# One stage program, a transfer in place of a shift matmul, and new engine orders in a local transformer on one Trainium2 core

## The reference, cut to what matters

```
def shift_tokens(t):
    a, s = jnp.split(t, 2, -1)
    s = jnp.pad(s, ((0, 0), (1, 0), (0, 0)))[:, :-1]
    return jnp.concatenate([a, s], -1)
...
for i in range(DEPTH):          # 6
    x = attn_layer(shift_tokens(x), Wqkv[i], q_scale[i], k_scale[i], Wo[i]) + x
    x = ffn_layer(shift_tokens(x), ln_g[i], ln_b[i], W1[i], b1[i], W2[i], b2[i]) + x
```

## Time and profile before

| what | value |
|---|---|
| median of 3 runs | 2609.49 us (2609.47 to 2609.76) |
| the profiled execution's own time | 2604.96 us |
| its span | 2603.1 us |
| PE busy in the span | 96% |
| DVE, ACT, POOL busy | 74%, 68%, 57% |
| granted TensorE clock, mean | 0.983 |

### The profile page before, as it was taken

How to read it: one execution, slowest core, us unless ns; L and a number is a source line. 1 busy time by engine, 2 the same in 40 slices (tenths; PEclk the granted TensorE clock), 3 DMA queues, 4 the chain that set the end, 5 groups by cost and what they waited for, 6 DMA issues and landing times.

```text
span 2603.1 us, 102870 instructions
## 1 busy us (share of the span) xinstructions
PE 2496.2 (96%) x41090; PEld 1928.4 (74%) x41090; DVE 1934.7 (74%) x4711; ACT 1771.4 (68%) x3770; POOL 1491.5 (57%) x1917
## 2 busy tenths in 40 slices
PE   8899999999999999999999999999799988999898
PEld 6667777777677777777677777777698967999667
DVE  6778788888878878788888878887456877555564
ACT  6677777777777778777777777777454357333465
POOL 5566677677666676676677677667332056000572
PEclk9999999999999999999999999999899989999999
DMA  3200000110011100110010100000002000000022
GB/s 94 67 19 12 16 16 15 33 32 21 19 26 29 32 19 19 32 34 17 19 33 25 29 19 16 14 16 16 4 5 88 0 5 6 2 0 1 13 78 82
DMA packets 56424, 66.72 MB, mean 26 GB/s; under 512 B 25113, under 2 KB 31076, under 8 KB 55652
## 3 DMA queue, kind: packets, MB, share of 16 engines
q1 hardware_dynamic: 56292, 64.88, 9.0%
HBM read 38.23 MB, written 1.05 MB: 15 GB/s over the span
## 4 chain that ended last, share of the span: by engine, by line
PE 85%; issue 5%; DVE 4%; POOL 4%; ACT 3%; DVEq 0%; DMA 0%; SPq 0%; POOLq 0%; ACTq 0%
PE ps L797 13%; PE ps L902 7%; PE ps L818 6%; PE ps L811 6%; PE ps L845 5%; PE ps L882 5%; PE ps L924 5%; PE ps L859 3%; PE ps L936 3%; PE ps L892 3%; PE ps L1016 3%; PE ps L1000 3%; PE ps L1001 3%; PE ps L742 2%; PE ps L752 1%
## 5 line engine op out<-in xcount | busy, mean ns | idle before, releaser
L1192 ACT ACTIVATE area<-ps 128x512 f32<-128x512 f32 (+4 forms) x1520 | 770.0, 536 | 380.2 <-PE ps L788 109.6
L1670 POOL TENSOR_TENSOR area<-area 128x512 f32<-128x512 f32 x384 | 481.9, 1276 | 8.2 <-DVE area L2149 8.2
L1692 POOL TENSOR_TENSOR area<-area,mx 128x512 f32<-128x512 f32 x192 | 200.2, 1043 | 489.2 <-DVE mx L2177 489.2
L797 PE MATMUL ps<-lw,area 128*128 128x512 f32 x768 | 413.2, 620 | 1.5 <-ACT area L1192 1.1
L1684 POOL TENSOR_TENSOR area<-area,rnq 128x512 f32<-128x512 f32 x384 | 392.5, 1043 | 7.5
L1315 ACT ACTIVATE area<-ps 128x512 f32<-128x512 f32 x384 | 227.1, 591 | 89.9 <-PE ps L797 89.8
L2147 DVE TENSOR_TENSOR area<-ps,table 128x512 f32<-128x512 f32 x384 | 260.9, 679 | 8.2 <-ACT area L1315 5.0
L2149 DVE TENSOR_TENSOR area<-ps,table 128x512 f32<-128x512 f32 x384 | 261.5, 681 | 0.0
L2128 DVE TENSOR_REDUCE ssq<-area 128x8 f32<-128x512 f32 x384 | 252.2, 677 | 1.7 <-ACT area L1315 0.8
L811 PEld LDWEIGHTS ps<-ident,area 128*128 128x128 f32 x1536 | 180.6, 142 | 65.0 <-issue 53.1
L811 PE MATMUL ps<-ident,area 128*128 128x128 f32 x1536 | 218.4, 275 | 10.6 <-POOL area L1684 7.7
(11 more groups left out here) (300 smaller groups left out, 5607.6 us busy)
## 6 DMA issues: line engine op xcount, KB each, us to landing
lvm<-area SPq DMA_DIRECT2D x384, 65.0 KB
lw<-in_wqkv SPq DMA_DIRECT2D x36, 256.0 KB
area<-in_moe_w SPq DMA_DIRECT2D x24, 256.0 KB, 2.7
lw<-in_wout SPq DMA_DIRECT2D x12, 256.0 KB
ctxT<-in_ctxT SPq DMA_DIRECT2D x64, 38.5 KB, 1.8
lw<-in_moe_w SPq DMA_DIRECT2D x8, 256.0 KB, 2.8
lw<-in_wff SPq DMA_DIRECT2D x6, 341.0 KB
lw<-in_moe_g SPq DMA_DIRECT2D x1, 1152.0 KB
```

Source lines behind the costliest of these rows:

```text
L797: nc.tensor.matmul(banks[:, lb_qk[j], :], xsT[s], wqkv[w.p][:, j * 512:(j + 1) * 512], start=True, stop=True).then_inc(l_qk_ps, 1)
L1192: return nc.scalar.activation(dst, src, ACT.Identity if kw else ACT.Copy, **kw)
L1670: pool.tensor_tensor(QR[s][:, cols], QR[s][:, cols], RA[s][:, cols], ALU.add).then_inc(l_rsum, 1)
```

## The change

It has five parts.

1. The token shift of the feed-forward half is no longer two matmuls. `y1` gets 64 more columns (`ysh`), and SP copies y1's features 64 to 127 of tokens 0 to 126 into these columns one partition lower: an SBUF to SBUF DMA of 127 rows of 256 bytes, which waits for y1. Row 0 is zeroed once.
2. The statistics read `ysh` in SBUF. The normalisation moves from DVE to ACT as one activation with scale 1/deviation and bias -mean/deviation; DVE makes that bias with a one-column instruction (`norm_shift`).
3. The orders in `stages` of PE, ACT, DVE and POOL and the PSUM banks are new; on POOL, `rotary_sum` and `normalised` of a unit move from its b call to its a call, as does `queries_keys_T` 2 on ACT.
4. The gated addition after the local transformer is split: sequences 0 and 1 first, the other 14 inside the first stage of the next attention.
5. Three of the `late_prep` instructions move ahead of the first mixture, behind a wait for all late loads; the preparations of w3 and w3o move into the last quad of the second mixture.

```
-        lb_tokens, lb_qk, lb_qkT, lb_v = 3, (4, 3, 4, 0), (3, 0, 2, 5), (1, 5)
+        lb_tokens, lb_qk, lb_qkT, lb_v = 0, (0, 7, 4, 2), (7, 6, 5, 7), (3, 6)
...
+        def shifted_tokens(s):
+            return ysh[s].rearrange("p (k n) -> p k n", n=64)[:, 0:3:2, :]
...
+            def shifted_tokens(s, unit):
+
+                sp.wait_ge(l_y1, unit + 1)
+                sp.dma_start(ysh[s][1:S, D:D + 64], y1[s][0:S - 1, 64:D]).then_inc(l_sh_ps, 16)
+
+            def stages(a, b, c):
+                if a:
+                    middle_values(*a)
+                    shifted_tokens(*a)
...
-            def shift_back(s, w):
-                pe.wait_ge(l_y1, nth(0, w.it, s))
-                nc.tensor.matmul(banks[:, lb_shift, 0:64], ident[:, :], y1[s][:, 0:64], start=True, stop=True)
-                nc.tensor.matmul(banks[:, lb_shift, 64:128], shift[:, :], y1[s][:, 64:128],
-                                 start=True, stop=True).then_inc(l_sh_ps, 1)
...
+            def shifted_normed(s, w):
+                act.wait_ge(l_nb, nth(0, w.it, s))
+                copy(xn[s][:, :].rearrange("p (k n) -> p k n", n=64), shifted_tokens(s), scale=rs[s][:, 0:1],
+                     bias=nrm[s][:, 0:1]).then_inc(l_xn, 1)
...
             def shifted_stats(s, w):
-                dve.wait_ge(l_sh_ps, nth(0, w.it, s))
-                V.bn_stats(st[s][:, 0:6], banks[:, lb_shift, 0:D]).then_inc(l_st, 1)
+                dve.wait_ge(l_sh_ps, 16 * nth(0, w.it, s))
+                V.bn_stats(st[s][:, 0:6], shifted_tokens(s)).then_inc(l_st, 1)
...
-            def shifted_normed(s, w):
+            def norm_shift(s, w):
+                dve.wait_ge(l_mv, nth(0, w.it, s))
                 dve.wait_ge(l_rs, nth(0, w.it, s))
-                V.tensor_scalar(xn[s][:, :], banks[:, lb_shift, 0:D], mv[s][:, 0:1], rs[s][:, 0:1],
-                                ALU.subtract, ALU.mult).then_inc(l_xn, 1)
+                V.scalar_tensor_tensor(nrm[s][:, :], mv[s][:, 0:1], -1.0, rs[s][:, :], ALU.mult, ALU.mult).then_inc(l_nb, 1)
...
+                    if b is None and c is None:
+                        gated(slice(G, B))
...
             attention(XA[1], 1)
-            mixture(MOE[0])
             dve.wait_ge(late_loaded, 288)
             V.tensor_tensor(side[:, :], side[:, :], side[:, :], ALU.add).then_inc(late_prep, 1)
...
+            mixture(MOE[0])
```

More of the change, by code:

```diff
@@ L543, in middle_values, with three @@
                     sp.dma_start(LVM[s][at + 32:at + 64, :, :], LV[s][at + 32:at + 64, 0, :, :]).then_inc(l_vm, 16)
-            def layer(l):
-                with sp.Fori(0, IT) as pr:
-                    for s in range(G):
-                        middle_values(s, l * B + pr * G + s)
+            def shifted_tokens(s, unit):
[5 more added lines that the diff above has]
+                    shifted_tokens(*a)
+            def three(s, unit):
+                stages((s, unit), (1 - s, unit - 1), (s, unit - 2))
             def layer_and_next_weights(l, p):
@@ L559, in layer_and_next_weights @@
                             sp.dma_start(dst, src).then_inc(lw_loaded[p], 16)
-            layer(0)
+            stages((0, 0), None, None)
+            stages((1, 1), (0, 0), None)
+            with sp.Fori(0, IT - 1) as pr:
+                for s in range(G):
+                    three(s, pr * G + G + s)
             with sp.Fori(0, DEPTH // 2 - 1) as lp:
@@ L564, in _ @@
                 layer_and_next_weights(lp * 2 + 2, 1)
-            layer(DEPTH - 1)
+            with sp.Fori(0, IT) as pr:
+                for s in range(G):
+                    three(s, (DEPTH - 1) * B + pr * G + s)
+            stages(None, (1, DEPTH * B - 1), (0, DEPTH * B - 2))
+            stages(None, None, (1, DEPTH * B - 1))
             contexts(1)
@@ L861, in probs_T, with probs_values @@
                 last.then_inc(l_pT_ps, 1)
[L863 removed]
+            def probs_values(s, w, m, near=None):
                 if m == 0:
@@ L987, in quad_logits, with output_shift, output_means @@
                 last.then_inc(r_lg_ps, 1)
+            def output_shift():
+                pe.wait_ge(m_rw, 2 * B - 3)
+                for c in range(4):
+                    last = nc.tensor.matmul(later[:, 0, 0:D], ob[:, c:c + 1].to_broadcast([D, S]), w3o[:, c, :], start=(c == 0), stop=(c == 3))
+                last.then_inc(t_prep_ps, 1)
+            def output_means():
+                pe.wait_ge(t_prep, 3)
+                for c in range(4):
+                    last = nc.tensor.matmul(later[:, 1, 0:D], mean512[:, :], w3o[:, c, :], start=(c == 0), stop=(c == 3))
+                last.then_inc(t_prep_ps, 1)
             def mixture(m):
@@ L1128, in stages @@
                     if b: outputs(*b)
-                def gain_sums():
-                    pe.wait_ge(t_prep, 3)
-                    for c in range(4):
-                        last = nc.tensor.matmul(ps[1][:, 2, 0:D], mean512[:, :], w3o[:, c, :], start=(c == 0), stop=(c == 3))
-                    last.then_inc(t_prep_ps, 1)
                 def up(b):
@@ L2232, in stages @@
                 if a: tokens(*a)
+                if b:
+                    masked(*b, 0)
+                    maxima(*b, 0)
                 if c:
@@ L2319, in halves @@
                         residual(*b)
+                        if m["n"] and ahead is None: output_weights(b[0])
                 dve.wait_ge(x_updated, G + m["ln"])
```

372 lines of the change are left out of this document (192 added, 180 removed).

## The result

The change makes the kernel 1.4% faster, a little under half of what was forecast: a median of 2573.63 us (2572.11 to 2573.84, 3 runs) against 2609.49, a ratio of 0.9863 (95% interval 0.985 to 0.9876), 35.9 us less. The forecast was 2533.

The account below looks back on a forecast made before the run. PE (TensorE) was taken to bound the local transformer's units: -0.53 - 0.29 + 0.05 = -0.77 us a unit, -73.2 over 95 distances; with the ends -76.8 in total, forecast 2533 us, range 2512 to 2572.

Parts of the forecast that it names:

- Two shift matmuls, -0.53: PE in the steady unit: removing the two shift matmuls saves their issue time, 0.53 us a unit.
- Tile shapes, -0.29: PE in the steady unit: fewer entries to and exits from small-tile groups save 0.29 us a unit, bounds 0 and -0.4.
- Waits, +0.05: PE in the steady unit: waits of 0.32 us after the change against 0.27 before, so +0.05 a unit.
- The two chains that I walked: PE's waits in the new order: probs_T 1 behind scores 1, 0.21 us; scores 0 behind queries_keys_T 0, 0.11 us.
- Loop ends and layer borders, which the change leaves alone: Local transformer: the 0.19 us by which the mean distance of 17.66 exceeds the 17.47 unit stays as it was.
- Transfer, 3.5 us, free: Shift DMA from y1 to shifted_stats: takes 3.5 us and costs nothing, since up to about 3.8 us is covered.
- SP's order, nothing: SP's queue: the four value transfers now wait behind the new transfer but still land in time for probs_values 0; no cost.
- Gated sum, -1.9: After the local transformer: 256 columns first instead of 2048, the other 14 sequences where DVE waits anyway; saves 1.9 us.
- Late preparations, +0.5: First mixture: DVE waits for late loads until 1995.5, net +0.5 us; bounds -1.4 (loads done in time) and +3.
- w3 and w3o, -2.2: Linear attention's start: preparations moved into the second mixture let key transposes start earlier, net -2.2 us; bounds +1 and -3.2.
- the signs named ahead: Local transformer: unit distances 16.7 us, landing near 3.5, DVE idle before statistics under 0.5; wrong if PE idle exceeds 60.
- The first rival, "the waits come back": Steady unit: PE's waits return in the tight order, only -0.40 us a unit gained, 2568 us; chance 0.17.

Follow-up runs that it names:

- a1_tokens_early: The changed kernel with DVE's wait for its own second_residual moved from ahead of tokens to ahead of masked 0: 2566.74 us, ratio 0.9834.
- a2_dve_unrolled: The changed kernel with DVE's inner loop over pairs of units written out: 2554.87 us, ratio 0.9792.
- a9_two_waits: The changed kernel with DVE's inner loop written out, its second_residual wait ahead of masked 0, queries_keys_T 0 between the halves of project: 2542.71 us, ratio 0.9748.
- a13_factors_early: a9_two_waits with POOL's loop written out and its next-layer rotary_factors one stage earlier, ahead of differences 0: 2536.02 us, ratio 0.9724.
- a14_old_order_unrolled: The kernel before, with only DVE's inner loop written out: 2592.47 us, ratio 0.9941.
- a4_shift_added: The changed kernel with two matmuls of the removed shift's shape, result unread, put in ahead of values 1: 2611.19 us, ratio 1.0003.
- a3_pv_apart: The changed kernel with the two probs_values groups taken apart again, up 0 standing between them: 2627.05 us, ratio 1.0062.
- a8_ends_undone: The changed kernel with gated sum, late preparations and w3/w3o preparations put back as in the kernel before: 2574.51 us, ratio 0.9864.
- a12_more_unrolled: a9_two_waits with the loops of ACT and POOL written out too: 2542.63 us.
- a6_shift_in_two: The changed kernel with the shift transfer cut into two pieces of 112 and 15 rows, DVE waiting for both: 2580.37 us, ratio 0.989.

## Why the prediction was wrong

The mechanism was right: TensorE bounds the unit, the two matmuls and the joined groups come off it, and the transfer is hidden. The step that failed is the sum "Together 0.32 against 0.27, +0.05" for the waits of PE: TensorE's idle time rose by 0.33 a unit. The edits that take waits away show that this is where the time went. Between the first and the last transpose of tokens, in us:

| kernel | time | PE busy | PE idle |
|---|---|---|---|
| before | 1677.8 | 1661.4 | 16.4 |
| the change | 1650.1 | 1602.1 | 48.0 |
| a1_tokens_early | 1641.7 | 1600.0 | 41.7 |
| a2_dve_unrolled | 1631.7 | 1601.1 | 30.7 |
| a9_two_waits | 1618.2 | 1600.9 | 17.3 |
| a13_factors_early | 1611.4 | 1600.4 | 11.0 |

From the change on the busy time stays within some 2 us while the time falls with the idle. Part of what they gain was to be had before the change too, 14.5 us by DVE's loop. The smaller part of the miss is the work taken off, 0.63 a unit by busy time for the forecast 0.82. By the prediction's own points:

- *Two shift matmuls, -0.53*: -0.53 by the rows of the old order (0.50 there with DVE's loop written out, a14_old_order_unrolled), -0.39 at another place of the new one (a4_shift_added). Read at 0.14 more than two such matmuls cost there.
- *Tile shapes, -0.29*: -0.53 in the sums by operation, 0.10 of which is the wait for y1, and the join alone 0.55 in the new order, waits included (a3_pv_apart). Too small, on the good side.
- *Waits, +0.05*: +0.76 in the rows of the table that got longer, +0.33 in idle time. The two chains that I walked are there: ahead of `scores` 0 a wait of 0.18 (forecast 0.11), and 0.13 ahead of `probs_T` 1 (0.99 against 0.86, forecast 0.21) with 0.10 more in the transposes themselves, whose weight loads are the ones that wait (PEld L878, 74.6 us in all). What was left out: `tokens` behind `second_residual` behind `down` (0.14 in even units by a1_tokens_early; in odd units `scores` 0 to `tokens_T` takes up to 1.33 where it is 0.78 with DVE's loop written out), the group ahead of `scores` 1 (1.07 for 0.95), `up` in two pieces (0.11). And of the 0.27 that I credited to the old order as waits that would vanish, only 0.10 is a wait that the rows show (for y1); 0.08 was DVE's back edge, and nothing shows that the rest was waiting. Nor could the walk be tested by giving 17.45 for the 17.47 of before: the 0.27 was what was left of 17.47.
- *"Loop ends and layer borders, which the change leaves alone"*: wrong. The distances exceed the shortest steady unit by 17.37 - 17.05 = 0.32 on the mean, before 0.19, 12 us in all. Half of it lies in the odd units, some 4 us by DVE's loop; the five borders, the outer loop's back edge and one of the first units have 2 each. A border unit itself is no longer than before, 18.65 against 18.70. POOL's factors there are what a13_factors_early got back, 7 us.
- *Transfer, 3.5 us, free*: 3.44, free. The cover is about 4.5, not 3.8. The first part of the walk was right (DVE is ready for the statistics 3.16 us after the issue, forecast 3.1); what lies behind them is more than the 0.8 taken. That the old order would not have hidden it was in no term, and is worth 2.8 us a unit.
- *SP's order, nothing*: no wait of TensorE for the values' transfers shows; splitting the new one, which adds an issue to SP, costs 7 us, but no run shows that SP's queue is the reason.
- *Gated sum, -1.9*: 1.8 at its place, but 0.5 net. The cover of the other 14 sequences was taken as free and isn't.
- *Late preparations, +0.5*: -1.4 by a8_ends_undone. DVE does not wait for the late loads at all: its three instructions run from 1968.08 to 1968.51 and the first product starts at 1968.42. The bound -1.4 was the truth: the loads were done in time.
- *w3 and w3o, -2.2*: -1.4 by a8_ends_undone, -2.8 by the traces of before and after. The wait of 3.39 is gone; in its place TensorE waits 2.46 for DVE's normalisation there:

```profile
2395.78 0.44 PE L1078 MATMUL ps<-ident,xn 128*128 128x128 f32 x1 [2.46 <-DVE xn L2387]
```

Of the signs named ahead, the landing and the idle of DVE ahead of the statistics (24.5 us in all) came as said, the distance of 16.7 did not, and PE's idle in the local transformer, 1615.00 - 1573.33 = 41.7 us, stayed under the 60 named as the mark of being wrong. That mark was badly chosen: the same reading of before gives 1645.00 - 1634.71 = 10.3, and the rise of 31 us is most of the 45 us by which the units missed. The mark had to be the forecast's own 0.05 a unit. The first rival, "the waits come back", named the right kind of cause and 2568.

What stays open: how the 0.11 ahead of `scores` 1 and the 0.13 of `probs_T` 1 could be had without breaking pairs, why the transfer in two pieces is slower, and what the 3 to 5 us at the outer loop's back edge are.

## What to carry to other kernels

When an order is packed tighter, don't price only the waits that you see coming: list for each engine which instruction now stands directly behind a wait, and follow each back to TensorE; the two that were taken out one by one here were worth 0.14 and 0.18 us a unit. Compare the idle time of the bounding engine with that of before, and not with a mark picked by feel. On TensorE equal groups belonged together here, and moving a group to fill a wait cost more than the wait. And it can be worth writing out a loop on an engine that looks idle for 3 us a unit: for VectorE it gave 15 to 19 us in both orders, for ScalarE and GpSimd nothing.

## What the runs showed of the hardware that I had not expected

- The back edge of VectorE's inner loop cost 0.3 to 0.5 us in every second unit of the change (17.33 to 17.54 against 17.05) and 0.2 to 0.4 in the old order (17.62 to 17.77 against 17.39), although VectorE is busy for only 14 of 17 us (a2_dve_unrolled, a14_old_order_unrolled). Those of ScalarE and GpSimd cost nothing (a12_more_unrolled).
- A transfer of 127 rows of 256 bytes from SBUF to SBUF lands 3.44 us after its issue, a second one right behind it 1.8 us later. If all of that is paid by the row, it is 1.8 / 127 = 14 ns a row (an estimate from these two). 112 and 15 rows in two transfers landed within 3.3 us of the first issue in most units (a6_shift_in_two).
- One more pair of changes between full and small tiles cost 0.55 us a unit, of which only 0.34 stand in the small groups themselves; the rest is spread over other groups and holds some waiting (a3_pv_apart).
- VectorE's wait for the semaphore of its own last instruction takes 0.25 us from that instruction's end to the start of the next (in the change, 996.62 + 0.29 to 997.16).
